# An attention stage and an FFN stage of one kernel: two blocks of code with a barrier become one, with the FFN's first layer put among the last attention pairs

## The reference

```
q = hidden_states @ Wq.T + bq
scores = q . memory_keys / sqrt(128)              # 8192 x 4096
mem_out = softmax(scores) @ memory_values
x = layernorm(x + mem_out @ Wo.T + bo)
h = silu((x @ w1.T) * w1_s) * ((x @ w2.T) * w2_s)  # 128 -> 512
h = gelu((h @ h1.T) * h1_s)                        # 512 -> 512
h = gelu((h @ h2.T) * h2_s)
x = layernorm(x + (h @ w3.T) * w3_s)               # 512 -> 128
```

## Time and profile before

| | |
|---|---|
| median of three runs | 1143.17 us (1141.53 to 1144.19) |
| the profiled execution | 1143.68 us |
| its span, first to last instruction | 1141.9 us, granted clock 0.995 of full |
| instructions | 20141 |
| PE busy | 96% |
| DVE, ACT, POOL busy | 84%, 79%, 57% |
| values of pair 31 end on PE | 772.0 us |
| turn 0 of the FFN begins on PE | 789.4 us |

### The profile page before, as it was taken

How to read it: one execution, slowest core, us unless ns; L and a number is a source line. 1 busy time by engine, 2 the same in 40 slices (tenths; PEclk the granted TensorE clock), 3 DMA queues, 4 the chain that set the end, 5 groups by cost and what they waited for, 6 DMA issues and landing times. The chain is left out here.

```text
span 1141.9 us, 20141 instructions
## 1 busy us (share of the span) xinstructions
PE 1092.9 (96%) x5324; PEld 769.4 (67%) x5324; DVE 963.5 (84%) x1803; ACT 905.3 (79%) x1610; POOL 645.3 (57%) x618
## 2 busy tenths in 40 slices
PE   7799999999999999999999999988999999999996
PEld 5566666666666666666666666635787887888775
DVE  6888898998899889998998899875787887888874
ACT  6788788878887887788878877777788878888883
POOL 1487788878877887888778878760211121121110
PEclk9999999999999999999999999999999999999999
DMA  6878888888888888888888988854020111001000
GB/s 199 190 186 200 200 201 205 206 197 204 201 195 195 202 200 199 200 206 202 200 194 208 207 186 198 186 124 166 1 56 28 28 48 34 28 28 55 11 10 29
DMA packets 83942, 165.90 MB, mean 145 GB/s; under 512 B 19648, under 2 KB 47808, under 8 KB 83776
## 3 DMA queue, kind: packets, MB, share of 16 engines
q1 hardware_dynamic: 79824, 161.50, 59.8%
q10 hardware_dynamic: 4080, 3.94, 1.2%
HBM read 22.76 MB, written 8.39 MB: 27 GB/s over the span
## 5 line engine op out<-in xcount | busy, mean ns | idle before, releaser
L454 POOL TENSOR_TENSOR pT<-slot_p,pT 128x512 f16<-128x512 f32 x496 | 561.9, 1168 | 143.5 <-ACT pT L506 143.5
L608 DVE TENSOR_SCALAR_CACHE_REDUCE rows<-s_ps 128x1024 f32<-128x1024 f32 x256 | 310.8, 1214 | 72.9 <-DMA slot_p<-rows 48.3
L506 ACT ACTIVATE pT<-slot_p 128x512 f16<-128x512 f32 x512 | 296.1, 617 | 84.1 <-DMA slot_p<-rows 76.2
L577 DVE STREAM_TRANSPOSE rows<-rows 128x1024 f32<-128x1024 f32 x256 | 317.0, 1239 | 2.1 <-ACT rows L497 2.1
L497 ACT ACTIVATE rows<-rows,bias 128x1024 f32<-128x1024 f32 x256 | 291.6, 1139 | 15.7 <-DVE bias L616 15.4
L711 PE MATMUL s_ps<-keys,q_buf 128*128 128x512 f32 x512 | 249.6, 488 | 7.7 <-DVE rows L608 4.8
L685 PE MATMUL o_ps<-pT,v_hi 128*128 128x512 f16 x512 | 198.1, 387 | 21.2 <-POOL pT L454 20.9
L990 PE MATMUL ring<-h_hi,w_all 128*128 128x512 f32 x512 | 205.6, 402 | 1.7 <-DVE h_lo L936 1.4
L712 PE MATMUL s_ps<-keys,q_buf 128*128 128x512 f32 x512 | 203.4, 397 | 0.0
L991 PE MATMUL ring<-h_lo,w_all 128*128 128x512 f32 x512 | 202.3, 395 | 0.0
L713 PE MATMUL s_ps<-keys,q_buf 128*128 128x512 f32 x512 | 202.1, 395 | 0.0
(11 more groups left out here) (95 smaller groups left out, 1202.1 us busy)
## 6 DMA issues: line engine op xcount, KB each, us to landing
slot_p<-rows SPq DMA_DIRECT2D x1020, 128.0 KB, 2.4
x_in<-in_xT SPq DMA_DIRECT2D x32, 128.0 KB, 2.5
x_in<-in_x SPq DMA_DIRECT2D x16, 256.0 KB, 3.6
o_scratch<-o_sum SPq DMA_DIRECT2D x32, 128.0 KB, 2.0
out<-y_out SPq DMA_DIRECT2D x16, 256.0 KB, 2.4
o_in<-o_scratch SPq DMA_DIRECT2D x14, 256.0 KB, 3.3
z<-in_w_all ACTq DMA_DIRECT2D x25, 113.0 KB, 3.1
rows<-in_w_all SPq DMA_DIRECT2D x1, 2816.0 KB, 12.5
```

What stands on the lines that cost most here:

```text
L454: nc.gpsimd.tensor_tensor(halves(s % RING, 1), slots_first(pp, s), halves(s % RING, 0), ALU.subtract).then_inc(split, 1)
L506: nc.scalar.activation(halves(s % RING, 0), slots_first(pp, s), ACT.Copy).then_inc(highed, 1)
L577: nc.vector.transpose(row_piece(tile, k), row_piece(tile, k)).then_inc(turned, 1)
L608: nc.vector.tensor_scalar(row_piece(tile, k), s_ps[:, j % 2, :], 1.0, None, ALU.mult, ALU.max, accum_out=part_max[:, tile, k:k + 1]).then_ ...
```

## The change

`attention` and `ffn` become one function `layers` with one `nc.Block()`, so the barrier between them is gone. `frames` ends with frame 31; what followed is written out by hand, engine by engine:

- PE: the values of pair 30, steps 0 to 11; first layer of block 0, chunks 0 and 1 (8 matmuls); the values of pair 30, steps 12 to 15; chunks 2 and 3; the values of pair 31; `turn_x1(1)`; the h1 layer of block 0; then turn 0. The branch on the weights stands before the values of pair 30.
- ACT: sends the last two pieces of pair 31 instead of one, after steps 11 and 14 of pair 30; loads the silu table after step 15; gates 0 and 1, their rounded products, `output_half(30)`; the high parts of pair 31 with gates 2 and 3 after steps 8 and 11, the gelu table and a rounded product after step 13.
- DVE: `split_x1(0)` before `residual(1)`; the low parts of pair 30 from step 12 on (`LATE_STEP`), products 0 and 1 and their low parts, then the low parts of pair 31 with `normalise_x1(1)`, products 2 and 3 and a low part between them; `output_sum(30)` and `(31)` after that.
- POOL: low parts of pair 30 to step 11 only; it takes over the branch that DVE had.
- SP: one piece fewer to send; the loads of o and x for blocks 2 and 3 (four DMAs of 256 KB) stand right behind its last piece, then it waits for all pieces of pair 31 and issues the 2816 KB load of the raw weights, and only then the stores of pairs 30 and 31.
- The buffer `prod` is gone: a product is written over its gate. For block 0 gates and products lie in `rows`, two places for four chunks. `h_hi[0]` and `h_lo[0]` lie in the keys.

```diff
-        for f in range(PAIRS - 4, PAIRS + 3):
+    for f in range(PAIRS - 4, PAIRS):
             frame(f, f % 2)
...
+    def product(b, j):
+        return rows[:, (2 + j % 2) * BT:(3 + j % 2) * BT] if is_step(b, 0) else gate[:, j, :]
...
 SP
-            sp.wait_ge(stage.xb_ready, 1)
-            sp.wait_ge(stage.y_done, 1)
-            stage.load_o(sp, 2, 0)
-            stage.load_x(sp, 2, 0)
+        exchange(PAIRS - 1, 1, 0, PIECES - 1)
+        exchange(PAIRS - 1, 1, 1, 0)
+        exchange(PAIRS - 1, 1, 1, 1)
+        stage.store_output(sp, PAIRS - 3)
+        for b in (2, 3):
+            sp.wait_ge(stage.xb_ready, b - 1)
+            sp.wait_ge(stage.y_done, b - 1)
+            stage.load_o(sp, b, b % 2)
+            stage.load_x(sp, b, b % 2)
+        for tile in range(2):
+            for k in range(PIECES):
+                sp.wait_ge(sent[tile][k], 16 * GROUPS * PAIRS)
+        sp.dma_start(raw, w_raw[:, 0:W_COLS]).then_inc(raw_loaded, 16)
+        stage.store_output(sp, PAIRS - 2)
+        stage.store_output(sp, PAIRS - 1)
...
 POOL
+        for s in range(STEPS - T_LAG, LATE_STEP):
+            low_part(PAIRS - 2, 0, s)
         stage.inverse_deviation(pool, 1, 0)
+        pool.wait_ge(stage.low_found, 1)
+        low = pool.value_load(stage.low_max[0:1, 0:1].bitcast(I32))
+        with pool.If(low > 0):
...
+        with pool.Else():
+            nc.gpsimd.memset(table_room[:, 1:2], 0.0).then_inc(w_split, 2)
...
 ACT
+        def gate_of(b, j):
+            act.wait_ge(in_done, 8 * b + 2 * j + 1)
+            at_least(act, in_split, j - 1 if is_step(b, 0) else 4 * b + j - 3)
...
+        for s in range(6, STEPS):
+            high_part(PAIRS - 2, 0, s)
+            if s == 7:
+                act.wait_ge(sent[0][0], 16 * GROUPS * PAIRS)
+                stage.keep_x1T(act, 0)
+            for k in (2, 3):
+                if s == (11, 14)[k - 2]:
+                    act.wait_ge(turned, 8 * (PAIRS - 1) + PIECES + k + 1)
+                    send(act, 1, 1, k)
+        load_table(ACT.Silu)
+        for k in (1, 2):
+            act.wait_ge(sent[0][k], 16 * GROUPS * PAIRS)
+        for j in range(2):
+            gate_of(0, j)
+        for j in range(2):
+            product_high(0, j)
+        stage.output_half(act, PAIRS - 2, 0)
+        for s in range(STEPS):
+            high_part(PAIRS - 1, 1, s)
...
 DVE
+        stage.split_x1(dve, 0)
+        for s in range(LATE_STEP, STEPS):
+            low_part(PAIRS - 2, 0, s)
+        stage.residual(dve, 1)
+        for j in range(2):
+            product_of(0, j)
+        for j in range(2):
+            product_low(0, j)
+        for s in range(STEPS):
+            low_part(PAIRS - 1, 1, s)
+            if s == 5:
+                stage.normalise_x1(dve, 1)
+            if s == 8:
+                product_of(0, 2)
+            if s == 11:
+                product_of(0, 3)
+            if s == 13:
+                product_low(0, 2)
+        product_low(0, 3)
+        stage.output_sum(dve, PAIRS - 2, 0)
+        stage.output_sum(dve, PAIRS - 1, 1)
+        stage.sum_rows(dve, READY_TILES, TILES, 1)
...
 PE
+        def last_values(low_weights):
+            for s in range(STEPS):
+                add_values(PAIRS - 2, 0, s)
+                if s == (STEPS - 1 if low_weights else FIRST_LAYER_STEP):
+                    pe.wait_ge(scores_moved, 8 * PAIRS)
+                    pe.wait_ge(stage.w_rounded, CHECKS)
+                    pe.wait_ge(stage.x1_split, 1)
...
+                    first_layer(0, (0, 1), low_weights)
+            first_layer(0, (2, 3), low_weights)
+            for s in range(STEPS):
+                add_values(PAIRS - 1, 1, s)
+            stage.turn_x1(pe, 1)
```

1337 lines of the change are left out of this document (665 added, 672 removed).

## The result

The changed kernel takes 1132.25 us (1130.21 to 1132.74, 4 runs) where the kernel before takes 1142.9 (1141.53 to 1144.19); the ratio is 0.9904, 95% interval 0.9886 to 0.9921. It is faster by 10.6 us where 4.0 were forecast. Its profiled execution took 1131.77 us, its span 1130.0.

What follows compares the result with a forecast made beforehand. PE, 96% busy, bounds the kernel; only the drain before turn 0 moves: 5.2 us added ahead of 772, more removed behind, shift -4.1. From 1143.7 to 1139.6, less 0.5 for the median, plus 0.1 for handoffs: 1139.2; range 1137.4 to 1142.4.

Steps and rivals of the forecast that it cites:

- Step 1: ACT in pair 30: two sends start at 749.5, issues 0.87 us each, high part 15 ends at 757.2.
- Step 2: DVE in pair 30: low part 15 done at 757.9, then residual(1) of 2.3 us, done at 760.2.
- step 5: Pair 31: DVE's string bounds, 13.0 us to 776.4; ACT has 11.7 and PE's 16 steps 10.6.
- Rival A: ACT's sends: issues get dearer beside SP's loads; 1140.2 at 0.99 us each, about 1142 at 1.25; chance 0.14.
- Rival B: Pair 31's last piece lands late, at 768 behind SP's loads, 5.3 us after the need; 1144.4; chance 0.06.
- D: Drain: nothing gained, DVE's low parts at overlapped price or fetch or another wait eats it; 1141.7; chance 0.10.
- C: PE's clock: 2 us idle ahead of pair 31 slows value steps, late costing 2 us; 1141.1; chance 0.10.
- The 1140.2 that the forecast gives for this rule: ACT's table switch: about 1.38 us of drain beside the 1.28 load would end gates 1.3 later; estimated 1140.2.
- about 1.6 of slow clock: PE behind 772: slow-clock time that goes away, beside 2.09 of barrier, 1.42 of wait and 16 first-layer matmuls.
- steady turns of the same length: FFN loop, new profile: turns keep their length; another length after turn 0 would prove the forecast wrong.
- the change leaves their order alone: Steady FFN turns: they are PE's and keep their order, so new time is old plus turn 0's shift.
- Gate j waits for a low part of the block before, long done: Products written in place of their gates: the gate's wait is already met, costed at nothing.

Runs made afterwards that it cites:

- the run with SP's sends: Changed kernel with the last two pieces of pair 31 sent by SP's queue again instead of ACT's: 1131.91 us, ratio 0.9905.
- the one it was made from: Changed kernel with h_hi1 to h_lo2 and the attention's tensors at multiples of 128 bytes, and in_done waited for ahead of gated: 1127.68 us, ratio 0.9868.

## Why the forecast was right and wrong

**The drain was right**, -4.1 against -4.2 to -4.3 in the profiled pair, and so were most of its steps. On the old clock (3.0 us added to the rows after):

```
step                                   forecast   measured
1  high part 15 starts / ends        756.6/757.2   755.0/755.6
2  residual(1) done                       760.2     760.3
3  first layer starts / ends        757.5/759.4     757.9/760.0
4  products 0 and 1 done                  761.6     761.6
   first high part of pair 31, ends       763.3     763.8
5  last low part of pair 31               776.4     776.6
6  last value step / turn 0        777.2/785.3      777.5/785.1
```

Two of them were right by errors that cancelled, and that was luck. Step 1 had high part 15 end 1.6 us too late. The first issue stands at 745.68 in the trace after, while high parts ahead of it in the program run until 748.7, so the sends began 0.8 us before the step's 749.5; and the eight issues took 5.97 us together, 0.75 each instead of 0.87. (The Trainium skill, Advanced Engine Details and Errata, section "Sequencer Loop", has engine instructions wait in a queue while the next ones are read; by that an issue can overtake the work that is still queued, and this trace agrees with its rows at 745.68.) What stands behind an issue does wait, as the step said: the last issue ends at 751.95 and high part 15 starts at 752.00. The profile puts that wait down to PE, but the values it needed had ended at 749.68. Step 2 gave low parts on DVE 0.68 us and one overlap of 0.5. All four ran beside POOL's, 5.67 us for four, 1.42 each; that took back what ACT had won. Two smaller errors cancelled behind them: the first high part of pair 31 ended 0.5 us late, because `output_half(30)` waited 0.51 for PE, and the string of step 5 was 0.3 us shorter than its 13.0.

Rival A (dearer issues) did not happen: one issue of the eight took 1.36 us, the others 0.61 to 0.79, and the run with SP's sends shows that nothing hung on them. Rival B did not either: in the changed kernel the last piece landed at 756.64, 3.5 us before the first high part of pair 31. D did not: low parts of pair 31 ran at 0.60. Of C only the old slow stretch is left. As for the table switches, the drain that the Trainium skill, ScalarE: Activation LUTs, section "What ACT_TABLE_LOAD costs", states is not there: the load starts 0.01 us behind high part 15, and the next instruction 0.01 behind the load. (The 1140.2 that the forecast gives for this rule is less than 1139.2 + 1.3; the slack in it is not worked out.)

One term of the sum is in part luck: the "about 1.6 of slow clock" that goes away behind the barrier. Of nine traces of kernels in the old order, five have full clock from the barrier to turn 0 (granted clock 1.00 behind the same wait of 2.1 to 2.2 us), and their inner drains are 38.5 to 38.8 us; the two of the kernel before have 39.5 and 40.1. In the new order six traces, that of the run with SP's sends among them, have 35.3 to 35.8. The gain is 3.3 us at full clock and up to 4.8 beside a slow stretch.

Step 5 called DVE's string the bound. Taking 3.5 us out of it brought h1 forward by 1.5 us against the changed kernel and by 1.9 against the one it was made from. So DVE is the bound, but only by about 1.5 us; the step had ACT's 11.7 behind DVE's 13.0, which agrees. That ACT is what comes next was not tried.

**What failed is the sentence "steady turns of the same length"**, and before it "the change leaves their order alone". The order was left alone, and I took order for time. Three terms were missing:

- 24 matmuls of h1 in `keys`: 0.2333 to 0.2269 once they run evenly, 0.13 us of a turn (6.04 to 5.91) and 0.02 in the first chunk. The prediction names the `keys` room nowhere; the difference in address was in the diff.
- Two waits of DVE's products that were long met: 0.17 us a turn. "Gate j waits for a low part of the block before, long done" looked at the waits that came, not at those that went.
- The turn at the loop's exit, 1.0 us, of which 0.3 are the two terms above and 0.7 are a stall. Every traced kernel of the old form had this stall (22.53 to 22.86 us against turns of 21.6 to 22.0), and none of the new form had it (21.42 to 21.67). The rows show four instructions of one kind stretched by 1.0 us and name nobody that they waited for. Why is open: no run tried whether it is the fetch of code behind the loop.

Together 12 turns of 0.28 and 1.0 make 4.4. With the drain and 0.2 at the end 8.9 us belong to the change. The rest to 10.6 is not located; the interval of the ratio, 9.0 to 13.0 us, begins just above 8.9.

The range, 1137.4 to 1142.4, had room for rivals of the drain and none for an effect outside it.

## What to carry to other kernels

Where an edit moves a tensor, reckon the distance between a matmul's moving operand and its weights, here modulo 256 bytes: 192 against 0 costs 2.8% of every matmul in a stage that TensorE bounds. Put the wait that is met last at the end of a row of waits, and count the waits that an edit takes away. Compare landmarks of two traces of the same kernel before giving a difference of 3 us to a change, and set them close around what was changed: from the last `q_buf` the drain of the changed kernel differed by 0.7 us between two runs, from the last transposes by 0.02.

## What the runs showed of the hardware

- The pace of back-to-back 128x512 fp32r matmuls, each with its own weight load, is 0.2269 to 0.2337 us, by the distance of the two addresses modulo 256, and VectorE and ScalarE at work beside them change nothing in it.
- Two waits already met, behind one that blocks, cost VectorE 0.11 to 0.17 us a turn, about 0.05 to 0.08 each.
- DMA issues on ScalarE's queue run beside its work that stands ahead of them (first issue at 745.68, high parts ahead of it until 748.7) and hold what stands behind them (751.95, then 752.00).
- 2.13 us of idle TensorE were followed by 3.3 us at a granted clock of 0.51. But the wait of 2.1 to 2.2 us at the barrier was followed by a granted clock of 1.00 in six of nine traces, so the length of an idle stretch alone does not decide it here.
- The end of the attention stage, 700 us long, differed by 0.5, 2.6 and 4.6 us between two runs of one kernel; the FFN stage repeats within 0.1 (288.67 and 288.64, 284.31 and 284.28).
